# Graph attention: 19 chunks of the edge gathers fetched row by row by SyncE and ScalarE instead of GpSimd

## What is computed

```python
xw = (x @ W).reshape(n, H, D)
a_src = jnp.einsum('nhc,hc->nh', xw, att_src)
a_dst = jnp.einsum('nhc,hc->nh', xw, att_dst)
logits = jax.nn.leaky_relu(a_src[src] + a_dst[dst], NEG_SLOPE)
m = jax.ops.segment_max(logits, dst, num_segments=n)
ex = jnp.exp(logits - m[dst])
s = jax.ops.segment_sum(ex, dst, num_segments=n)
alpha = ex / (s[dst] + EPS)
msg = xw[src] * alpha[..., None]
out = jax.ops.segment_sum(msg, dst, num_segments=n).mean(axis=1) + bias
```

## Time and profile before

| | |
|---|---|
| median of 3 runs | 7308.85 us (7306.36 to 7349.27) |
| profiled execution | 7287.62 us, span 7285.8 us |
| GpSimd busy | 4430.9 us (61%), 4689 gathers of about 0.94 us |
| PE, DVE, ACT busy | 3973.7, 3732.6, 2921.3 us (55%, 51%, 40%) |
| DMA | 444.78 MB, mean 61 GB/s |
| granted TensorE clock | 0.58 of full speed |

### The profile page before, as it was taken

How to read it: one execution, slowest core, us unless ns; L and a number is a source line. 1 busy time by engine, 2 the same in 40 slices (tenths; PEclk the granted TensorE clock), 3 DMA queues, 4 the chain that set the end, 5 groups by cost and what they waited for, 6 DMA issues and landing times. The chain is left out here.

```text
span 7285.8 us, 87026 instructions
## 1 busy us (share of the span) xinstructions
PE 3973.7 (55%) x21983; PEld 3698.6 (51%) x21983; DVE 3732.6 (51%) x9512; ACT 2921.3 (40%) x5694; POOL 4430.9 (61%) x4701
## 2 busy tenths in 40 slices
PE   4444445454444355555555555545666666666666
PEld 4444444444444344444444444444666666666666
DVE  4333333333333344444444444446777777777777
ACT  2222222222222144444444444444555555555555
POOL 4666666666666556666666666645666666666663
PEclk6555555555555555555555555555555555555555
DMA  5322222222222122222222222222222222222221
GB/s 118 64 52 52 52 52 52 54 52 52 52 52 52 42 54 55 55 55 55 55 55 54 55 55 56 56 55 66 75 74 74 74 74 76 74 74 74 74 74 48
DMA packets 354021, 444.78 MB, mean 61 GB/s; under 512 B 142024, under 2 KB 233574, under 8 KB 353360
## 3 DMA queue, kind: packets, MB, share of 16 engines
q0 software_dynamic: 150112, 217.86, 16.0%
q10 hardware_dynamic: 50400, 132.89, 5.2%
q1 hardware_dynamic: 153424, 93.06, 5.0%
HBM read 407.90 MB, written 39.55 MB: 61 GB/s over the span
## 5 line engine op out<-in xcount | busy, mean ns | idle before, releaser
L1076 POOL DMA_INDIRECT rows<-tab,idx_now x4653 | 4392.7, 944 | 2765.6 <-issue 1631.1
L1383 DVE TENSOR_SCALAR share_prev<-psum,prev_all 128x4 f32<-128x4 f32 x258 | 57.2, 222 | 2253.1 <-remote 2244.9
L2088 PE MATMUL psum<-share,rows 128*65 128x132 f32 (+10 forms) x6240 | 1181.3, 381 | 0.0
L2183 PE MATMUL psum<-own,hot_t 112*128 112x64 f32 x3126 | 697.0, 422 | 859.3 <-DVE mix L1549 734.5
L2183 PEld LDWEIGHTS psum<-own,hot_t 112*128 112x128 f32 x3126 | 674.8, 330 | 887.1 <-issue 646.2
L2088 PEld LDWEIGHTS psum<-share,rows 128*65 128x65 f32 x6240 | 1096.4, 224 | 5.7
L1753 ACT ACTIVATE sums<-psum 65x448 f32<-65x448 f32 x260 | 140.1, 539 | 2053.1 <-remote 2044.0
L2199 PE MATMUL psum<-hot,prob 128*128 128x112 f32 x3126 | 667.8, 406 | 33.4 <-issue 28.8
L2115 PE MATMUL psum<-w_next,turned 65*112 65x72 f32 x262 | 83.4, 421 | 1079.2 <-ACT turned L1757 1079.1
L2199 PEld LDWEIGHTS psum<-hot,prob 128*128 128x128 f32 x3126 | 647.5, 317 | 32.6 <-issue 27.7
L2115 PEld LDWEIGHTS psum<-w_next,turned 65*112 65x112 f32 x262 | 58.0, 281 | 1115.7 <-ACT turned L1757 940.1
(11 more groups left out here) (246 smaller groups left out, 6549.5 us busy)
## 6 DMA issues: line engine op xcount, KB each, us to landing
rel_t<-rel_row ACTq DMA_DIRECT2D x256, 336.0 KB
rows<-tab,idx_now POOLq DMA_INDIRECT x4653
rel_t<-rel_runs ACTq DMA_DIRECT2D x128, 336.0 KB
own<-tab SPq DMA_DIRECT2D x262, 63.0 KB
cut<-cut_row SPq DMA_DIRECT2D x130, 120.2 KB
tab<-row SPq DMA_DIRECT2D x131, 112.0 KB
tab<-row SPq DMA_DIRECT2D x131, 63.0 KB
own<-tab SPq DMA_DIRECT2D x131, 56.0 KB
```

The source lines that it names most:

```text
L1076: nc.gpsimd.indirect_dma_start(rows_of[p][:, G * c.s + j, 0:D] if raw else rows_of[p][:, G * c.s + j, :], None, x if raw else halves[p], b ...
L2088: done = nc.tensor.matmul(summed[:, :, LO[j]:HI[j]], rows_g[:, at + j, 0:D + 1], of[:, j, :, 0:SUBS[j]], start=not opened, stop=j == chunk ...
L2183: done = nc.tensor.matmul(added3[:, j, :], hot_t[k][:, P * j:P * j + P], own3[c.s][:, 0:D], start=True, stop=True)
```

## The change

In passes 0 and 1 the gathers of 19 chunks, all 12 of unit 123 and the first 7 of unit 124, are no longer issued by GpSimd. Their 128 x 19 rows are fetched by plain DMAs of one row of 71 floats each, half of the rows (partitions 0 to 63) by SyncE and half by ScalarE. One iteration of the hardware loop fetches one chunk: each of its six units issues 10 or 11 of an engine's 64 rows, after the engine has loaded the 10 or 11 row numbers from SBUF into registers (`side_src`, refilled by a DMA at the end of the iteration). On SyncE this stands in the unit between `fetch_cuts` and `store`, on ScalarE between `row_turn` and `strip_of`. The rows land in `side_rows`, the space of a buffer that only pass 2 uses. `strip_of` and `sums_of` read the two units from there (`chunk_rows`), in unit 122 to 124 the copies of `strip_of` are split accordingly, and the landing counts of the ring are corrected (`came_aside`). Five semaphores are folded into others to make room. Pass 2 is as before.

```diff
@@ -104,6 +104,10 @@
 
     RAW = 3
 
+    SIDE, SIDES = NU - 8, (NU - RING) // RING - 1
+    SIDE_W = 71
+    assert G < SIDES < 2 * G and GW <= SIDE_W <= HALF
+
     SPREADS = [0, RING, 36, 68, 100, NU]
 
     def landed(p, c, each, tail, each3=None, tail3=None):
@@ -114,13 +118,18 @@
...
+    def came_aside(p, c, count):
+
+        return sum(count(m) for before in range(2) for u, m in ((SIDE, G), (SIDE + 1, SIDES - G))
+                   if u % RING == c.s and (before < p or before == p and c.at_least(u)))
+
     def first_landed(p, c):
 
-        return landed(p, c, 1, 1, 2, 2)
+        return landed(p, c, 1, 1, 2, 2) - 16 * came_aside(p, c, lambda m: 1)
 
     def rest_landed(p, c):
 
-        return landed(p, c, G - 1, LASTC - 1, G - 2, LASTC - 2)
+        return landed(p, c, G - 1, LASTC - 1, G - 2, LASTC - 2) - 16 * came_aside(p, c, lambda m: m - 1)
 
     def chunks(c):
         return LASTC if c.at_least(NU - 1) else G
@@ -506,6 +514,20 @@
...
+
+
+        side_rows = prob3[0][:, :, :].rearrange("p c d -> p (c d)")[:, 0:SIDES * HALF].rearrange("p (c w) -> p c w", w=HALF)
+
+        def beside(c):
+
+            if not c.at_least(SIDE) or c.at_least(SIDE + 2):
+                return 0
+            return SIDES - G if c.at_least(SIDE + 1) else G
+
+        def chunk_rows(c, j):
+            if j < beside(c):
+                return side_rows[:, G * (c.u - SIDE) + j, :]
+            return rows_g[:, G * c.s + j, :]
@@ -854,6 +876,27 @@
...
+        def fetch_side_src(eng, i, k):
+
+            h = P // 2
+            eng.dma_start(side_src[0:1, h * i:h * i + h],
+                          src[bass.ds(UE * SIDE + P * k + h * i, h)].rearrange("(p e) -> p e", p=1))\
+                .then_inc(side_src_in[i], 16)
+
+        def fetch_side_rows(eng, i, p, c):
+
+            k, h = c.q - 1, P // 2
+            r0, r1 = [h * i + h * (c.s + b) // RING for b in range(2)]
+            if c.s == 0:
+                eng.wait_ge(side_src_in[i], 16 * (c.q + (SIDES + 1) * p))
+                eng.sem_inc(go, 1)
+            _, nodes = nc.values_load_multi_w_load_instructions(side_src[0:1, r0:r1], engines=(eng.engine,))
+            for r, node in zip(range(r0, r1), nodes):
+                eng.dma_start(side_rows[r:r + 1, bass.ds(k, 1), 0:SIDE_W].rearrange("p a w -> p (a w)"),
+                              tab[p][bass.ds(node, 1), HALF:HALF + SIDE_W]).then_inc(side_in[p], 16)
+            if c.s == RING - 1:
+                fetch_side_src(eng, i, k + 1)
+
@@ -1007,8 +1050,13 @@
                 sp.wait_ge(most_ready, NU * p + 1)
                 sp.sem_inc(go, 1)
                 fetch_cuts(p, unit(2))
+                if p > 0:
+                    sp.wait_ge(side_src_in[0], 16 * p * (SIDES + 1))
+                if p < 2:
+                    fetch_side_src(sp, 0, 0)
                 for c in units(sp):
                     n = NU * p + c.u
+                    aside = p < 2 and not isinstance(c.q, int)
                     if p == 1:
                         run = rel_row[bass.ds(UE * c.u, 1)].offset
                         sp.dma_start(bass.AP(rel_runs.tensor, run, [[P, chunks(c)], [QUAD, RUNS], [1, QUAD]]),
@@ -1020,12 +1068,14 @@
                         if p == 0 and c.below(4) and c.at_least(3):
                             sp.wait_ge(cut_spread, 16 * (len(SPREADS) - 1))
                         fetch_cuts(p, c.plus(3))
+                    if aside:
+                        fetch_side_rows(sp, 0, p, c)
...
@@ -1072,12 +1122,12 @@
                     if p == 2 and not c.below(RING):
                         pool.wait_ge(own3_ready, c.u - 3)
                     pool.sem_inc(go, 1)
-                    for j in range(chunks(c)):
+                    for j in range(beside(c) if p < 2 else 0, chunks(c)):
                         nc.gpsimd.indirect_dma_start(rows_of[p][:, G * c.s + j, 0:D] if raw else rows_of[p][:, G * c.s + j, :],
                                                      None, x if raw else halves[p],
                                                      bass.IndirectOffsetOnAxis(ap=idx_now[:, c.s, j:j + 1], axis=0))\
                             .then_inc(first_in[c.s] if j < (2 if p == 2 else 1) else rows_in[c.s], 16)
-            pool.wait_ge(end_ready, 1)
+            pool.wait_ge(prep_step, 65)
             for k, u in enumerate((FULL - 1, FULL)):
                 n = 2 * NU + u
                 pool.wait_ge(row_kept_v, n + 1)
@@ -1690,22 +1738,32 @@
 
             def strip_of(p, c):
 
-                n, at = NU * p + c.u, G * c.s
-                a_src = rows_g[:, :, D + 1:GW]
-                act.wait_ge(rows_in[c.s], rest_landed(p, c))
-                act.wait_ge(first_in[c.s], first_landed(p, c))
+                n, at, m = NU * p + c.u, G * c.s, chunks(c)
+                heads_of = slice(D + 1, GW)
+                if beside(c.plus(1)) > beside(c):
+                    act.wait_ge(side_in[p], 16 * P * SIDES)
+                if beside(c) < m:
+                    act.wait_ge(rows_in[c.s], rest_landed(p, c))
+                if beside(c) == 0:
+                    act.wait_ge(first_in[c.s], first_landed(p, c))
                 if not (p == 0 and c.below(1)):
                     act.wait_ge(strip_used, n)
                 if not c.below(1):
-                    before = G * c.plus(-1).s + G - 1
-                    nc.scalar.activation(strip[:, 0, :], a_src[:, before, :], ACT.Copy).then_inc(strip_ready, 1)
+                    nc.scalar.activation(strip[:, 0, :], chunk_rows(c.plus(-1), G - 1)[:, heads_of], ACT.Copy)\
+                        .then_inc(strip_ready, 1)
                 else:
                     act.sem_inc(strip_ready, 1)
-                m = chunks(c)
-                nc.scalar.activation(strip[:, 1:m + 1, :], a_src[:, at:at + m, :], ACT.Copy).then_inc(strip_ready, 1)
+                b = beside(c)
+                if b > 0:
+                    first = G * (c.u - SIDE)
+                    copied = nc.scalar.activation(strip[:, 1:b + 1, :], side_rows[:, first:first + b, heads_of], ACT.Copy)
+                if b < m:
+                    copied = nc.scalar.activation(strip[:, b + 1:m + 1, :], rows_g[:, at + b:at + m, heads_of], ACT.Copy)
+                copied.then_inc(strip_ready, 1)
                 if not c.at_least(NU - 1):
-                    act.wait_ge(first_in[c.plus(1).s], first_landed(p, c.plus(1)))
-                    nc.scalar.activation(strip[:, G + 1, :], a_src[:, G * c.plus(1).s, :], ACT.Copy)\
+                    if beside(c.plus(1)) == 0:
+                        act.wait_ge(first_in[c.plus(1).s], first_landed(p, c.plus(1)))
+                    nc.scalar.activation(strip[:, G + 1, :], chunk_rows(c.plus(1), 0)[:, heads_of], ACT.Copy)\
                         .then_inc(strip_ready, 1)
                 else:
                     act.sem_inc(strip_ready, 1)
@@ -1821,11 +1879,16 @@
                         raw_coefs(u)
                 strip_of(p, unit(0))
                 raise_logits(p, unit(0))
+                if p > 0:
+                    act.wait_ge(side_src_in[1], 16 * p * (SIDES + 1))
+                fetch_side_src(act, 1, 0)
                 for c in units(act, TAIL):
                     if not c.below(1):
                         keep_sums(p, c.plus(-1))
                     if not c.below(2):
                         row_turn(p, c.plus(-2))
+                    if not isinstance(c.q, int):
+                        fetch_side_rows(act, 1, p, c)
                     strip_of(p, c.plus(1))
                     one_hots_turned(p, c.plus(2))
                     if not c.below(2):
@@ -2070,14 +2134,13 @@
...
+                    nc.tensor.matmul(summed[:, :, 0:1], chunk_rows(c.plus(-1), G - 1)[:, 0:D + 1], of_prev[:, :].unsqueeze(2),
                                      start=True, stop=False, skip_group_check=True)
                     opened = True
                 for j in range(chunks(c)):
@@ -2085,7 +2148,7 @@
...
-                    done = nc.tensor.matmul(summed[:, :, LO[j]:HI[j]], rows_g[:, at + j, 0:D + 1], of[:, j, :, 0:SUBS[j]],
+                    done = nc.tensor.matmul(summed[:, :, LO[j]:HI[j]], chunk_rows(c, j)[:, 0:D + 1], of[:, j, :, 0:SUBS[j]],
```

More of the change, by code:

```diff
@@ L249, in build @@
         row_out = [sb_over_x(f"row_out{k}", [W, D]) for k in range(2)]
-        sb_over_x("rest_of_x", [P, 1520])
+        side_src = sb_over_x("side_src", [1, P], I32)
+        sb_over_x("rest_of_x", [P, 1520 - P])
         rows = sb_over_x("rows", [P, RING * G * 2 * D])
@@ L413, in build @@
         idx_staged = sem("idx_staged")
+        side_in = [sem(f"side_in{p}") for p in range(2)]
+        side_src_in = [sem(f"side_src_in{i}") for i in range(2)]
         first_in = [sem(f"first_in{s}") for s in range(RING)]
@@ L889, in _ @@
             for t in range(3):
-                sp.dma_start(tab[t][N:NT, :], zeros[0:NT - N, 0:tab[t].shape[1]]).then_inc(table1_out, 16)
```

(15 more changed lines are left out.)

7 lines of the change are left out of this document (removed).

## The result

The changed kernel takes 8800.1 us (8782.5 to 8810.0) against 7309.0 us: a ratio of 1.202, 95% interval 1.198 to 1.207, 1491 us more. Its profiled execution has a span of 8780.5 us. The forecast was slower, 8070 us, in a range of 7250 to 8800 us: the direction is right, the loss is nearly twice the forecast one, and the time lies at the very top of the range.

The account below looks back on a forecast made before the run. The prediction took a cycle of waits, 18.0 us a unit, as the bound, no engine being busy over 61%. 228 units x 3.5 us = 798 us, less 34, gave 764 us more: about 8070 us, range 7250 to 8800.

Parts of the forecast that it names:

- The bound: Whole loop: a unit of 18.0 us is one burst of gathers, 2.6 us until TensorE's signal, 0.8 us to the next.
- Skipped gathers, 34 us: GpSimd, units 123 and 124 of passes 0 and 1: 38 gathers fewer save 34 us, range 34 to 54.
- A row, 0.47 us, and one load, 2.5 us: SyncE and ScalarE, unheld: issuing one row takes 0.47 us, loading a unit's row numbers 2.5 us (0.5 to 5.5).
- SyncE, 20.3 us a unit in pass 0: SyncE's slowed instruction queue sets the unit: 20.3 us in pass 0, 21.1 in pass 1; cut and own fetches queue behind rows.
- ScalarE, even at 323 ns: ScalarE is not slowed during bursts: its fetch costs 323 ns each time in the loop.
- TensorE's turn of the strip is held by about 4 us: ScalarE's route: rows delay the strip's turn, whose signal is held about 4 us; the unit becomes 21 us.
- The sum: Both routes act together: 21.5 us a unit, 3.5 more; 228 units give 798 us, less 34: 764 us more.
- Two routes to 20.3 and 21 us: SyncE's used-up queue gives 20.3 to 21.1 us a unit, ScalarE's rows on the chain 21 us.
- What would show it: Signs in the new profile: fewer gathers per 500 us, SyncE's row DMAs near 0.7 us, no SyncE gap, a late scan.
- All hidden: Rival, chance 0.30: SyncE's slowness is waiting and ScalarE's work fits beside the burst; 7255 to 7275 us.
- Hold to the end of the burst: Rival, chance 0.12: TensorE's signals are held to every burst's end; 25.5 us a unit, 8985 us.

Follow-up runs that it names:

- split: Changed kernel with only SyncE fetching single rows in pass 0, only ScalarE in pass 1; other half one DMA a chunk: 8241.5 us against 7294.2.
- sync_rows: Changed kernel with only SyncE fetching single rows; ScalarE sends one DMA of 64 fixed rows a chunk: 5946.9 us, ratio 0.9939 to the kernel before.
- none: Changed kernel without single-row fetches; each engine sends one DMA of 64 fixed rows a chunk: 5945.2 us, ratio 0.9938 to the kernel before.
- scalar_rows: Changed kernel with only ScalarE fetching single rows; SyncE sends one DMA of 64 fixed rows a chunk: 6409.1 us, ratio 1.071 to the kernel before.
- scalar_moved: Changed kernel with only ScalarE fetching single rows, in pass 1 moved behind row_front; SyncE one DMA a chunk: 8102.8 us against 7225.2.

## Why the prediction was right, and where it was off

The prediction had the direction and the places where the time goes; its size was off by nearly a factor of two (761 us forecast, 1491 measured), and that the time still lies at the top of the range, which ended at 24.5 us a unit, is luck: pass 0 stayed under that and pass 1 went over it.

- **The bound** (one burst, 2.6 us until TensorE's signal, 0.8 us): right for chips with slow stretches. It is not the kernel's alone: on the other kind a unit is 15.0 us. The prediction had one chip and could not know.
- **Skipped gathers, 34 us**: they gave 38 us on a chip without slow stretches; with them the ends of the passes gave back only 13.
- **A row, 0.47 us, and one load, 2.5 us**: right. 0.44 to 0.46 us where nothing holds it, and 2.5 us for eleven numbers; with the shorter loads of ten the mean is 2.1 us.
- **SyncE, 20.3 us a unit in pass 0**: right for SyncE alone, 20.55 by split, and there SyncE waits for no one from 500 to 2600 us, as forecast. (The sum has a slip: 39 and 43 instructions at 0.2 us are 7.8 and 8.6 us, not 8.2 and 9.0, so it should have said 19.9 and 20.7.) The way was another than the one named. The prediction put `cut` and `own` behind the rows; it was the store, which ScalarE waits for, and then TensorE's held turn. In the changed kernel SyncE does not set the unit: from 500 to 2900 us it waits for ScalarE's and VectorE's parts of the row for 253 us in 77 waits. One cost was missing: SyncE's loop is longer, and the step back to its start, once in six units, takes longer. In sync_rows SyncE's branch (L563) starts at 1055.9 and its next instruction at 1058.5, where it is 1054.4 and 1054.7 in none, and the queue of instructions moved 233 packets instead of none's 50. The Trainium skill ("Runtime: NRT & Kernel Launch", Instruction fetch mechanics) says that a taken branch out of a window of two pages of 256 instructions has to fetch its target first. The trace agrees for SyncE, whose loop of six units went from 116 recorded instructions to 313, but not plainly for ScalarE: in scalar_rows its loop has 325, and the next instruction still comes 0.24 us after the branch.
- **ScalarE, even at 323 ns**: this step failed. (Its rows and load are 5.0 + 2.5 = 7.5 us by the forecast's own terms, not 7.3; that changes nothing.) The earlier trace rows showed ScalarE only in the first microseconds of a burst, where it had its one fetch. With rows it is still issuing when the slow stretch begins, and slows down like SyncE.
- **TensorE's turn of the strip is held by about 4 us**: this failed too, for this route. In the unit above the turn starts at 1102.81, right after the copies, and the scan follows at 1103.75, and so in every unit of both passes. The hold is real, but it showed only on the other route, in split's pass 0. The two errors nearly cancelled in pass 0: 21 us forecast for this route, 20.36 measured (scalar_moved). In pass 1 they did not: 24.12 (split).
- **The sum** failed most. Two routes to 20.3 and 21 us were taken as one, "they act together, so I take 21.5", which puts what the second engine adds at next to nothing. Measured, its rows cost as much beside the other's as alone: in pass 0 18.0 + 2.5 + 2.5 = 23.0, measured 22.81. Taken as a sum with the forecast's own terms, pass 0 would have been 18.0 + 2.3 + 3.0 = 23.3 us. In pass 1 ScalarE's rows alone cost 6.1 us and both 8.5; what SyncE's alone cost there was not measured, so whether they add in pass 1 is open. Nor is it two late pieces one behind the other: SyncE's rows make ScalarE's part longer by 2.5 us in pass 0 and by 3.4 in pass 1, so that the sum comes out so closely may be chance. The loss a unit is 4.8 and 8.6 us instead of 3.5.
- **What would show it**: the gathers 1.25 us apart, the 38 fewer, 260 of them in 500 us of pass 0 and 331 in pass 2 came as named. Three signs did not come. SyncE's row DMAs have a median of 0.238 us, not 0.7, for most of them are issued outside a slow stretch and the time goes into the few that are not. SyncE still waits. And the scan follows the turn at once.
- **All hidden** (0.30): right without slow stretches for SyncE, false for ScalarE there (464 us), false for both with them. The Trainium skill ("DMA: Bandwidth & Descriptors", SWDGE vs HWDGE vs iDMA) says that DMAs issued by these two engines never touch the rings into which GpSimd writes its descriptors. No run here shows whether these rings have a part in it. What the traces show is that it is not a matter of DMAs alone: register steps that issue none take 0.7 us as well.
- **Hold to the end of the burst** (0.12, 25.5 us a unit): pass 1 came out at that length and beyond, but by ScalarE's rows and not by TensorE's signals.

What stays open: what distinguishes the two kinds of chip, and whether it is the chip at all or its state at the time, since each was met at one time only; and what it is that SyncE, ScalarE and TensorE's signals share in a slow stretch. The runs show only that it comes some microseconds into a burst of gathers and that breaks in the burst shorten it.

## What to carry to other kernels

Price what a second engine's work adds apart from what the first's adds, and do not take the larger of two routes for both without a row that shows that one hides the other: here it was nearer to the sum, since the two engines slowed each other down. An even duration in a trace holds only for the time within the cycle in which the engine was seen; before giving it more work, look at what the other engines suffer at the time when the new work would run. Where two chips differ by a fifth on one kernel, a change of 0.5% needs its comparison on one chip, or a stage in the same trace that the change doesn't touch.

## What the runs showed of the hardware

- One kernel takes 7225 to 7331 us on four chips and 5976 and 5983 us on two, with gathers 1.249 us apart on both.
- Some microseconds into a burst of gathers, SyncE and ScalarE go down to one instruction in about 0.7 us on chips of the first kind, register moves too. With rows on both engines each gets through 1.02 to 1.09 steps in a us from 9 to 15 us into a burst; alone ScalarE gets through 1.3 to 1.7 and SyncE 1.3.
- TensorE's signal of a finished turn, given 6.4 us into a burst, reached VectorE 10.7 us later (split, pass 0); in the changed kernel none took over 0.5 us.
- Two breaks in a burst of twelve, each 1.5 us longer than the usual 0.3, take most of the hold off TensorE's signal of the sums (from 8.6 to 3.2 us on average); with two breaks 0.7 us longer the unit stays as long as without.
- SyncE's step back to the start of its loop took 2.5 us with 313 recorded instructions in the loop and 0.2 us with 116.
- One load of ten row numbers into registers took 1.1 to 1.2 us, one of eleven 2.5 to 2.6 us.
